# A recommendation kernel: every fourth early row gather waits for VectorE's count of products

## The chip, the cores and the metric

One core of one Trainium2 chip. The metric is the device time of one execution in microseconds (us). In the rows PE is TensorE, DVE VectorE, ACT ScalarE, POOL GpSimd, SP SyncE. The count of products is a semaphore, a counter that engines raise and wait for.

## What is computed

Rows of 32 embedding tables are gathered for 512 samples (32 fields of 16 numbers each), three layers of a compressed interaction network run on them, and a small tower of three matrix products follows. All is float32.

```python
e = jnp.stack([tbl_0[ids[:, 0]], ..., tbl_31[ids[:, 31]]], axis=1)      # 512 x 32 x 16
x0, xk, outs = e, e, []
for W in (W0, W1, W2):                                                  # 32 x 32 x 64, then 32 x 64 x 64
    xk = relu(einsum('bmd,bhd,mhk->bkd', x0, xk, W))
    outs.append(sum(xk, axis=2))
h = concatenate([concatenate(outs, axis=1), dense_ctx], axis=1)         # 512 x 208
h = maximum(h @ W_top1 + b_top1, 0)
h = maximum(h @ W_top2 + b_top2, 0)
y = h @ W_top3
```

## The kernel before

The batch is cut into eight pairs of 32-sample chunks; pair 0 is cut further, so that there are ten blocks (`BLOCKS`, line 32): blocks 0 and 1 have 256 columns (sample times dimension), block 2 has 512, blocks 3 to 9 have 1024. A step is (layer, block), and `BEGUN` (line 53) lists the 30 steps in the order in which they are begun. The program is written by hand for each engine, with semaphores between them.

GpSimd fetches the rows. One gather (`gather`, line 590) is one indirect DMA that brings 128 table rows of 16 numbers, one for each partition; 128 of them bring everything, 16 for each pair. Block 0 needs gathers 0 to 3, block 1 gathers 4 to 7, block 2 gathers 8 to 15, block 3 gathers 16 to 31, block 4 gathers 32 to 47, block 5 gathers 48 to 63, block 6 gathers 64 to 79. `gathered` has room for four pairs (`GRING`), so gather 64 waits for the last products of layer 0 on pair 0 (product 26, line 598). GpSimd issues 32 gathers at once (line 638) and then, by `GATHERS_IN` (line 70), 41 more ahead of its first multiplication, so gathers 0 to 72 stand one behind the other with no other wait than that of gather 64. Gathers 73 to 78 follow that first multiplication (`opposite_product` of block 4), and later ones are strewn between GpSimd's own products (line 631).

SyncE issues the plain DMAs in the order of `LOADS` (line 86). `scratch(b)` waits for the gathers of block b and copies their rows to DRAM (line 509); `field_tiles(b)` brings them back as eight tiles of four fields each, spread over partitions (line 557), which layers 1 and 2 multiply with. `layer0_operands(b)`, for blocks 4 to 9 only, brings the own and the rotated tiles for layer 0 (lines 522, 528, 535). `LOADS` has the copy and operands of block 5 ahead of the field tiles of block 4.

VectorE makes the products: one instruction multiplies one to three tiles by a factor (line 683; for layer 0 of blocks 0 to 3, called direct, lines 694 to 706) and writes them to `vz`, a ring of nine tiles. `VECTOR` lists all 139 products in order, and each raises `vz_ready` by one. "Product 4" is the one that raises it to 4. Products 1 to 4 are layer 0 of block 0, 5 to 8 layer 0 of block 1, 9 to 22 layer 1 of these two blocks, 23 to 26 layer 0 of block 2, 27 to 40 layer 2 of blocks 0 and 1, 41 to 47 layer 1 of block 2, 48 to 52 layer 0 of block 3, 53 to 59 layer 2 of block 2, 60 to 65 layer 1 of block 3, 66 and 67 layer 0 of block 4, which are the first on `rotated`. Product 73 is the first of layer 0 of block 5, product 75 the first that multiplies with the field tiles of block 4.

TensorE contracts the products with the weights (line 881) and raises `vz_used`, for which VectorE waits before it writes over a tile. For the first blocks TensorE also makes the factors. For the direct blocks it spreads the gathered rows over partitions in two waves (`spread_gathered`, line 848), between which it waits for a semaphore of its own, `wave_done`; it raises `factor_spread`, for which ScalarE (copy to `own`, line 754) and VectorE wait. For layers 1 and 2 it spreads the ReLU that ScalarE made of the accumulator (lines 826 and 779). There are three factor buffers.

Of the kernel before, what the change touches and what calls it, by code (L numbers as in the profile page):

```python
# [37 lines left out]
def stream(b):  # L38
    return BLOCKS[b][0] % STREAMS
# [7 lines left out]
def turn(b):  # L47
# [22 lines left out]
GATHERS_IN = {(0, 4): (41,), (2, 3): (6, 0), (0, 5): (5,), (1, 4): (0, 1, 3, 0, 0), (1, 5): (4, 0),  # L70
              (0, 6): (4,), (2, 4): (0, 1, 2, 1), (0, 7): (1,), (2, 5): (7, 0, 1, 0), (1, 6): (0, 0, 3),
              (1, 7): (1, 8), (2, 6): (4, 3, 0, 0, 0)}


SPLIT = {8: (3, 3, 2), 7: (3, 2, 2), 6: (3, 3), 5: (3, 2), 4: (2, 2), 3: (3,), 2: (2,)}
# [37 lines left out]
def pool_units(step):  # L113

    layer, b = step
    if layer == 0:
        return [(0, L0TILES)] if b not in DIRECT else []
    return [(1, t) for t in range(TILES - POOL_TILES[step], TILES)]
# [60 lines left out]
def vectors_to(step):  # L179

    return max(i for i, (of, _) in enumerate(VECTOR) if of == step) + 1
# [77 lines left out]
def pools_to(step):  # L259

    return max([i + 1 for i, (of, _) in enumerate(POOLS) if of == step], default=0)


def pools_used_to(step):
    return max([i + 1 for i, (of, _) in enumerate(POOLS_USED) if of == step], default=0)
# [81 lines left out]
def cin_dlrm(nc, table, ids, first_row, unit, turned, across, w0a, w0b, w0c, w1, w2, wt1, bt1, wt2,  # L347
             bt2, wt3, wt1_dense, dense, out):
    with ExitStack() as ctx:
# [6 lines left out]
        def sem(name):  # L356
            return ctx.enter_context(nc.semaphore(name))
# [60 lines left out]
        vz_ready, vz_used = sem("vz_ready"), sem("vz_used")  # L418
# [21 lines left out]
        def hidden_of(step, g):  # L440
            _, col, cols, _, _ = BLOCKS[step[1]]
            return hidden[stream(step[1])][:, g, col:col + cols]
# [9 lines left out]
        def quarter_rows(b):  # L452

            pair, _, _, first, rows = BLOCKS[b]
            return gathered[:, pair % GRING, first:first + rows, :].rearrange("p b d -> p (b d)")

        def operands_in(b):

            return 16 * sum(1 for a in range(b + 1) if a not in DIRECT and stream(a) == stream(b))

        def landed(b):

            return 16 * (turn(b) + 1)

        def relay_count(step):

            return 32 * sum(1 for of in BEGUN[:BEGUN.index(step) + 1] if of not in SPREAD and of[0]
                            and stream(of[1]) == stream(step[1]))
# [119 lines left out]
        @block.gpsimd  # L588
        def _(pool):
            def gather(i):  # L590
                pair, j = divmod(i, GATHERS)
                b = next(b for b, (of, _, _, first, rows) in enumerate(BLOCKS)
                         if of == pair and first <= j < first + rows)
                if j == 0 and pair >= GRING:
                    before = max(a for a in range(len(BLOCKS)) if BLOCKS[a][0] == pair - GRING)
                    for a in range(before):
                        if BLOCKS[a][0] == pair - GRING:
                            pool.wait_ge(vz_ready, vectors_to((0, a)))
                    pool.wait_ge(scratch_in[stream(before)][0], landed(before))
                    if before in DIRECT:  # L600
                        pool.wait_ge(vz_ready, vectors_to((0, before)))
                    else:
                        pool.wait_ge(scratch_in[stream(before)][1], operands_in(before))
                        pool.wait_ge(pz_ready, pools_to((0, before)))
                nc.gpsimd.indirect_dma_start(  # L605
                    gathered[:, pair % GRING, j, :], None, table,
                    bass.IndirectOffsetOnAxis(ap=index[:, i:i + 1], axis=0)).then_inc(rows_in[b], 16)

            def opposite_product(step):
                _, col, cols, _, _ = BLOCKS[step[1]]  # L610
                s, quarter = stream(step[1]), cols // QUART
                pool.wait_ge(opposite_in[s], operands_in(step[1]))
                if step[1] - 1 not in DIRECT:
                    pool.wait_ge(pz_used, pools_used_to((0, step[1] - 1)))
                nc.gpsimd.tensor_tensor(oz[:, 0:quarter], quarter_rows(step[1]), opposite[s][:, :],
                                        ALU.mult).then_inc(pz_ready, 1)

            def product(step, u):
                _, col, cols, _, _ = BLOCKS[step[1]]
                s = stream(step[1])  # L620
                g, t = pool_units(step)[u]
                if step[0] == 1:
                    pool.wait_ge(fields_in[s][t], landed(step[1]))
                if u == 0 and step in SPREAD:
                    pool.wait_ge(hidden_copied, COPIED.index(step) + 1)
                elif u == 0:
                    pool.wait_ge(relayed[s][g], relay_count(step))
                at = PLANE.index((step, u))
                if at >= PRING:
                    pool.wait_ge(pz_used, PRODUCT_USED[at - PRING])  # L630
                nc.gpsimd.tensor_tensor(pz[:, at % PRING, 0:cols], fields[s][:, t, col:col + cols],  # L631
                                        hidden_of(step, g), ALU.mult).then_inc(pz_ready, 1)

            pool.wait_ge(ids_in, 32)
            nc.gpsimd.tensor_tensor(index[:, :], ids_sb[:, :], first_sb[:, :].broadcast_to([P, PAIRS * GATHERS]),
                                    ALU.add).then_inc(index_ready, 1)
            pool.wait_ge(index_ready, 1)
            for i in range(FIRST_GATHERS):
                gather(i)
            sent = FIRST_GATHERS  # L640
            for step, u in POOLS:
                if step in GATHERS_IN:
                    for i in range(sent, sent + GATHERS_IN[step][u]):
                        gather(i)
                    sent += GATHERS_IN[step][u]
                if step[0] == 0:
                    opposite_product(step)
                else:
                    product(step, u)
            assert sent == PAIRS * GATHERS, sent  # L650
# [379 lines left out]
```

## Time and profile before

| | us |
|---|---|
| median of three runs | 450.08 (448.92 to 450.79) |
| the profiled execution | 448.99 |
| its span in the profile | 447.2 |
| TensorE busy with matmuls | 319.0 (71%), 1824 instructions |
| VectorE busy | 283.7 (63%), 174 instructions |
| GpSimd busy | 244.4 (55%), 189 instructions |
| ScalarE busy | 53.0 (12%), 71 instructions |

The span is what the profile's clock covers of the profiled execution; 1.8 us of the execution lie around it. No engine is busy all the time, so the share of busy time alone says little: one has to ask in which stretch an engine stands still, and for whom. In the profile a stretch on the chain that is called "issue" has no releaser that the records show, and "another core or an unknown queue" or "remote" stands where a semaphore moved late with no instruction beside it.

### The profile page before, as it was taken

What the parts mean: (1) busy time and instruction counts of PE and PEld (TensorE: products, weight loads), DVE (VectorE), ACT (ScalarE), POOL (GpSimd) and SP (SyncE); (2) the same over time, 40 slices, a digit from 0 to 9 for tenths busy, and PEclk for the clock granted to TensorE, in tenths of its full rate; (3) what the DMA queues carried; (4) which work ended last, traced back from release to release, by engine and by line L of the source; (5) the groups of instructions that cost most, each with busy time, mean ns of one, the idle gap of its engine ahead of it and who ended that gap; (6) DMA issues with size and microseconds to landing.
All of it is one profiled execution on the core that took longest, in us unless ns stands there. A gap on an engine that the chain in (4) does not pass through costs nothing.

```text
span 447.2 us, 4701 instructions
## 1 busy us (share of the span) xinstructions
PE 319.0 (71%) x1824; PEld 135.9 (30%) x1824; DVE 283.7 (63%) x174; ACT 53.0 (12%) x71; POOL 244.4 (55%) x189
## 2 busy tenths in 40 slices
PE   0300003039922999889899999899889996999997
PEld 0200002037611643423233333233223442333334
DVE  0000000006702767999999997999899976899911
ACT  1000000000000010101112212220112221122002
POOL 5777777300174000003887688997887928887300
PEclk9999999999985799999999999999999998999999
DMA  5434484000070004760387868979875899934000
GB/s 174 106 100 110 107 286 128 4 1 1 30 241 13 1 0 119 268 238 7 92 279 264 297 166 297 331 183 284 255 194 150 252 366 349 310 95 106 1 0 0
DMA packets 33104, 69.40 MB, mean 155 GB/s; under 512 B 5818, under 2 KB 14138, under 8 KB 33082
## 3 DMA queue, kind: packets, MB, share of 16 engines
q1 hardware_dynamic: 22074, 55.46, 37.6%
q10 hardware_dynamic: 6912, 12.59, 10.1%
q0 software_dynamic: 4096, 1.06, 2.6%
q8 instruction: 14, 0.23, 0.2%
q14 instruction: 8, 0.07, 0.0%
HBM read 54.40 MB, written 1.84 MB: 126 GB/s over the span
## 4 chain that ended last, share of the span: by engine, by line
PE 29%; issue 20%; DVE 17%; DMA 16%; another core or an unknown queue 10%; POOL 5%; SPq 1%; DVEq 1%; ACT 0%; ACTq 0%
PE acc L881 19%; DVE vz L683 16%; DMA fields_sb<-fields 10%; PE factor L848 4%; POOL gathered L605 3%; DMA fields<-gathered 2%; PE factor L826 2%; POOL pz L631 2%; DMA gathered<-in_table,index 2%; DMA rotated<-fields 1%; DVE feats L713 1%; PE factor L931 1%; SPq L557 1%; PE factor L913 1%
## 5 line engine op out<-in xcount | busy, mean ns | idle before, releaser
L881 PE MATMUL acc<-vz,w_sb 128*64 128x512 f32 (+2 forms) x1240 | 231.2, 512 | 34.0 <-DVE vz L683 18.7
L683 DVE TENSOR_TENSOR vz<-fields_sb,factor 128x3072 f32<-128x3072 f32 (+5 forms) x110 | 231.1, 2144 | 36.3 <-remote 18.8
L631 POOL TENSOR_TENSOR pz<-fields_sb,hidden 128x1024 f32<-128x1024 f32 x50 | 117.7, 2376 | 96.1 <-ACT hidden L762 67.8
L605 POOL DMA_INDIRECT gathered<-in_table,index x128 | 121.8, 952 | 73.4 <-DVE vz L683 37.3
L881 PEld LDWEIGHTS acc<-vz,w_sb 128*64 128x64 f32 x1240 | 87.6, 144 | 163.6 <-issue 118.4
L700 DVE TENSOR_TENSOR vz<-own,factor 128x256 f32<-128x256 f32 (+2 forms) x10 | 7.9, 794 | 75.5 <-issue 30.1
L848 PE MATMUL factor<-gathered,turned_sb 32*128 32x64 f32 (+2 forms) x128 | 15.7, 393 | 55.8 <-issue 51.7
L881 PE MATMUL acc<-pz,w_sb 128*64 128x512 f32 x200 | 50.2, 593 | 1.3 <-POOL pz L631 1.3
L748 ACT ACTIVATE factor<-hidden 128x1024 f32<-128x1024 f32 x24 | 24.6, 1027 | 89.4 <-DMA hidden<-relu_out 56.7
L779 ACT ACTIVATE relu_out<-acc 128x512 f32<-128x512 f32 (+2 forms) x30 | 15.3, 510 | 151.3 <-PE acc L881 110.1
L848 PE MATMUL factor<-gathered,unit_sb 32*128 32x64 f32 (+2 forms) x32 | 5.1, 407 | 33.6 <-remote 20.8
L848 PEld LDWEIGHTS factor<-gathered,turned_sb 32*128 32x128 f32 x128 | 10.8, 251 | 60.0 <-issue 53.2
L683 DVE TENSOR_TENSOR vz<-rotated,factor 128x2048 f32<-128x2048 f32 x12 | 26.9, 2280 | 2.3 <-issue 2.3
L881 PEld LDWEIGHTS acc<-pz,w_sb 128*64 128x64 f32 x200 | 15.1, 137 | 29.4 <-issue 25.0
L713 DVE TENSOR_REDUCE feats<-relu_out 128x32 f32<-128x512 f32 (+2 forms) x30 | 17.1, 571 | 5.0 <-ACT relu_out L779 5.0
L704 DVE TENSOR_TENSOR vz<-own,factor 128x512 f32<-128x512 f32 (+1 forms) x3 | 2.6, 863 | 22.7 <-remote 22.4
L754 ACT ACTIVATE own<-factor 128x256 f32<-128x256 f32 (+2 forms) x4 | 2.4, 598 | 108.0 <-PE factor L848 73.5
L848 PEld LDWEIGHTS factor<-gathered,unit_sb 32*128 32x128 f32 x32 | 3.2, 244 | 35.3 <-remote 21.0
L826 PE MATMUL factor<-relu_out,unit_sb 32*128 32x128 f32 (+2 forms) x64 | 11.6, 468 | 0.6 <-issue 0.6
L748 ACT ACTIVATE factor<-own 128x1024 f32<-128x1024 f32 x6 | 6.2, 1028 | 27.9 <-issue 20.3
L826 PEld LDWEIGHTS factor<-relu_out,unit_sb 32*128 32x128 f32 x64 | 5.3, 206 | 6.6 <-issue 6.3
L877 PE MATMUL acc<-oz,w0c_sb 128*64 128x256 f32 x48 | 6.3, 379 | 0.0
(34 smaller groups left out, 50.9 us busy)
## 6 DMA issues: line engine op xcount, KB each, us to landing
fields_sb<-fields SPq DMA_DIRECT2D x56, 512.0 KB
rotated<-fields SPq DMA_DIRECT2D x24, 512.0 KB
hidden<-relu_out ACTq DMA_DIRECT2D x48, 256.0 KB
own<-fields SPq DMA_DIRECT2D x6, 512.0 KB
gathered<-in_table,index POOLq DMA_INDIRECT x128
fields_sb<-fields SPq DMA_DIRECT2D x16, 128.0 KB
fields_sb<-fields SPq DMA_DIRECT2D x8, 256.0 KB
fields<-gathered SPq DMA_DIRECT2D x13, 128.0 KB
```

The lines of the kernel that those rows point to most:

```text
L557: sp.dma_start(fields[s][:, t, col:col + cols], each).then_inc(fields_in[s][t], 16)
L605: nc.gpsimd.indirect_dma_start(gathered[:, pair % GRING, j, :], None, table, bass.IndirectOffsetOnAxis(ap=index[:, i:i + 1], axis=0)).then ...
L631: nc.gpsimd.tensor_tensor(pz[:, at % PRING, 0:cols], fields[s][:, t, col:col + cols], hidden_of(step, g), ALU.mult).then_inc(pz_ready, 1)
L683: nc.vector.tensor_tensor(vz[:, at:at + nt, 0:cols].rearrange("p t (a n) -> p t a n", n=half), src[:, t:t + nt, col:col + cols].rearrange( ...
L700: nc.vector.tensor_tensor(vz[:, at, 0:cols].rearrange("p (a n) -> p a n", n=half), whole, slot_of(step, t), ALU.mult).then_inc(vz_ready, 1)
L713: nc.vector.tensor_reduce(feats[layer][:, pair, first:first + count], relu_of(step).rearrange("p (b d) -> p b d", d=DIM), op=ALU.add, axis ...
L748: nc.scalar.activation(factor_of(step, g), src.rearrange("p (a n) -> p a n", a=2), ACT.Copy).then_inc(factor_put, 1)
L779: nc.scalar.activation(relu_of(step), acc[:, n % 2, 0:half], ACT.Relu).then_inc(relu_done, 1)
L826: last = nc.tensor.matmul(factor_of(step, g)[:, ab, :], unit_sb[row:row + HROWS, :], relu_of(before)[row:row + HROWS, :], start=True, stop ...
L848: last = nc.tensor.matmul(slot_of(step, held)[:, ab, wave * quarter:(wave + 1) * quarter], by, rows[row, :], start=True, stop=True)
L877: last = nc.tensor.matmul(acc_of(step, q // 2)[:, part], w0c_sb[:, q, :], quarters, start=False, stop=q % 2 == 1)
L881: last = nc.tensor.matmul(acc_of(step, ab), w_sb[layer][:, kt, :], z[:, ab * half:(ab + 1) * half], start=start and j == 0, stop=stop and ...
```

## The change

A table `PACED` is added. In `gather`, ahead of the indirect DMA, GpSimd waits for VectorE's count of products where the gather's number is in the table: gather 12 for product 4, 16 for 7, 20 for 14, and so on to gather 68 for product 61. The order of all instructions stays.

```diff
+PACED = {12: 4, 16: 7, 20: 14, 24: 18, 28: 22, 32: 29, 36: 35, 40: 41, 44: 44, 48: 47, 52: 49, 56: 54, 60: 57, 64: 59,
+         68: 61}
 ...
                     else:
                         pool.wait_ge(scratch_in[stream(before)][1], operands_in(before))
                         pool.wait_ge(pz_ready, pools_to((0, before)))
+                if i in PACED:
+                    pool.wait_ge(vz_ready, PACED[i])
                 nc.gpsimd.indirect_dma_start(
                     gathered[:, pair % GRING, j, :], None, table,
                     bass.IndirectOffsetOnAxis(ap=index[:, i:i + 1], axis=0)).then_inc(rows_in[b], 16)
```

## Rows read from the trace of the kernel before

**Rows 1.** Page part 2: busy tenths in 40 slices of 11.2 us each.
```profile
PE   0300003039922999889899999899889996999997
...
DVE  0000000006702767999999997999899976899911
...
POOL 5777777300174000003887688997887928887300
```

**Rows 2.** Chain of work, in order of time: start us, us, what.
```profile
19.68 51.69 issue
...
75.21 20.79 another core or an unknown queue
...
122.89 11.83 another core or an unknown queue
134.78 8.46 another core or an unknown queue
```

**Rows 3.** Timeline of PE, ACT and DVE, 18 to 97 us: start, us, what, idle before.
```profile
18.56 1.12 PE L848 MATMUL factor<-gathered,turned_sb 32*128 32x64 f32 x12 [3.61 <-remote]
71.37 0.69 PE L848 MATMUL factor<-gathered,turned_sb 32*128 32x64 f32 x4 [51.69 <-issue]
...
96.04 0.48 PE L848 MATMUL factor<-gathered,unit_sb 32*128 32x64 f32 x2 [20.83 <-remote]
...
36.49 0.38 ACT L754 ACTIVATE own<-factor 128x256 f32<-128x256 f32 x1 [34.46 <-issue]
...
59.76 0.69 DVE L704 TENSOR_TENSOR vz<-own,factor 128x512 f32<-128x512 f32 x1 [22.35 <-remote]
```

**Rows 4.** Instructions of line 605, of 0 to 84, 121 to 141, 237 to 243 us.
```profile
L605 POOL DMA_INDIRECT gathered<-in_table,index x64: 940/945/1112, 4.1 to 83.0; - x64
...
L605 POOL DMA_INDIRECT gathered<-in_table,index x15: 943/947/985, 121.3 to 139.4; - x15
...
L605 POOL DMA_INDIRECT gathered<-in_table,index x4: 946/948/985, 237.8 to 241.6; - x4
```

**Rows 5.** Timeline of DVE: products 5 and 8, 30, 31, 59 to 61, 73 and 74.
```profile
97.69 0.42 DVE L700 TENSOR_TENSOR vz<-own,factor 128x256 f32<-128x256 f32 x1 [9.66 <-ACT own L754]
...
101.88 0.21 DVE L694 TENSOR_TENSOR vz<-gathered,factor 128x64 f32<-128x64 f32 x1
...
122.86 0.69 DVE L683 TENSOR_TENSOR vz<-fields_sb,factor 128x512 f32<-128x512 f32 x1 [0.57 <-PE acc L877]
134.74 0.95 DVE L683 TENSOR_TENSOR vz<-fields_sb,factor 128x768 f32<-128x768 f32 x1 [11.20 <-remote]
143.26 0.95 DVE L683 TENSOR_TENSOR vz<-fields_sb,factor 128x768 f32<-128x768 f32 x1 [7.56 <-remote]
...
182.65 7.74 DVE L683 TENSOR_TENSOR vz<-fields_sb,factor 128x1024 f32<-128x1024 f32 x3
...
223.54 4.47 DVE L683 TENSOR_TENSOR vz<-rotated,factor 128x2048 f32<-128x2048 f32 x2
```

**Rows 6.** Windows: length, PE, PEld, DVE, ACT, POOL busy, clock, DMA share, GB/s.
```profile
84.00:96.00 12.00, 0.00 (x0) 0.00 (x0) 0.55 (x2) 0.00 (x0) 0.00 (x0) 1.00 0.00 1
...
106.00:121.00 15.00, 14.28 (x192) 10.72 (x188) 11.20 (x18) 1.17 (x4) 0.00 (x0) 1.00 0.01 3
...
143.30:151.00 7.70, 6.73 (x56) 5.60 (x56) 5.39 (x9) 0.28 (x1) 0.00 (x0) 0.53 0.01 2
151.00:190.50 39.50, 35.70 (x262) 16.94 (x262) 32.86 (x28) 3.59 (x6) 0.00 (x0) 1.00 0.34 112
```

**Rows 7.** Timeline of DVE beside short rows of gathers: products 77 to 80, 104.
```profile
235.65 12.07 DVE L683 TENSOR_TENSOR vz<-fields_sb,factor 128x2048 f32<-128x2048 f32 x4
...
316.24 3.35 DVE L683 TENSOR_TENSOR vz<-fields_sb,factor 128x3072 f32<-128x3072 f32 x1 [1.35 <-DMA fields_sb<-fields]
```

**Rows 8.** Timeline of SP's queue: rotated tiles of block 5, field tiles of block 4.
```profile
173.91 6.07 SPq L535 DMA_DIRECT2D rotated<-fields  x4
...
183.94 11.05 SPq L557 DMA_DIRECT2D fields_sb<-fields  x8
```

## The prediction

> **What bounds the kernel now.** I read the page's 40 slices first [rows 1]. The reader is to see that TensorE and VectorE are nearly empty in the first nine slices (0 to 100 us), thin again in the slices around 130 us, and full from about 150 us to the end, while GpSimd is busy in just the empty places. The second view is the chain of work [rows 2]: it names four stretches in which nothing on the chain works: 51.69, 20.79, 11.83 and 8.46 us, together 92.8 us of the 447.2 us span. The third is the timeline of those stretches [rows 3]. Block 0 has its rows early, and TensorE finishes the 12 spreading matmuls for products 2 and 3 at 19.68 us. But ScalarE's copy, which waits for the spread done before those, starts at 36.49 us, VectorE's product 2 at 59.76 us, and TensorE itself goes on at 71.37 and 96.04 us. All these wait for a count that TensorE raised long before: 40 us before, for product 2.
>
> What runs meanwhile is the row of gathers. 64 are issued back to back from 4.1 to 83.0 us, one each 1.25 us (79 us over 63 steps), and 15 more from 121.3 to 139.4 us [rows 4]. The second row of gathers brings the second standstill: product 30 starts at 122.86, product 31 at 134.74, product 32 at 143.26 us [rows 5]. TensorE's signals come through only some time after the gathers end: 96.04 minus 83.9 is 12.1 us after 80 us of gathers, 143.26 minus 140.4 is 2.9 us after 19 us of them, in both cases 15%. In the first of these tails, 84 to 96 us, neither DMA nor any engine is busy [rows 6], so it isn't the loads. And in 151 to 190.5 us, where there are loads (112 GB/s) but no gather, TensorE is busy 35.7 of 39.5 us [rows 6]. So I read: a long unbroken row of gathers holds back what TensorE signals to the other engines and to itself. From 151 us on the kernel is bound by VectorE and TensorE together, and whatever the first 61 products gain should move to the end.
>
> **The change part by part.** It adds 15 waits on GpSimd, ahead of gathers 12, 16, ... 68, and removes nothing. Behind each wait on GpSimd's queue stand all later gathers and, behind gather 72, the first opposite product. The long row of 64 becomes a row of 12, then 15 groups: 14 of four and a last of eleven (68 to 78). Each group starts when VectorE has finished product 4, 7, 14, ... 61. The wait as an instruction I price at nothing: GpSimd has idle time after every group.
>
> I add up when product 61 ends; before, that is 182.65 + 7.74 = 190.4 us [rows 5].
> - Until product 4: gather 11 ends at 4.1 + 11 x 1.25 + 0.95 = 18.8 us; a tail of 15% of 15 us gives 21.0. Then ScalarE's copy and products 1 to 4, whose spreads are half made. The same four products of block 1 take from 97.69 to 102.09, 4.4 us with the spreads between [rows 5]; I take 3.5. Product 4 ends at 24.5 us.
> - Products 5 to 61 without gathers: 96.04 [rows 3] to the stall at 122.9 is 26.5 us, 143.26 to 190.4 is 47.1 us, and products 30 and 31 between need some 3.5 us (two of 0.7 and 0.95 us and the ReLU between): 77 us.
> - The groups. One has four issues, 5.0 us, with its tail 5.75 us. The upper bound is 5.75: every signal held from the first gather to the tail's end and nothing running beside it. For the lower bound I look at short rows of gathers later on: the four at 237.8 to 241.6 us [rows 4] fall into a run of four products without a gap [rows 7], so their price is nothing, and eight from 310 us cost 1.35 us before product 104 [rows 7]. Those products last 3.3 us and the ring of nine tiles holds three of them; the early ones last 0.7 to 1.2 us, so VectorE has only some 2 to 3 us of work in stock. A group should cost between 5.75 - 2.45 = 3.3 us where products are short, and 2.2 us from the blocks of 512 columns on, if the signals are held throughout; I take these. Two groups (products 4 and 7), where everything hangs on TensorE's spreads, get 3.5 each. 7 + 5 x 3.3 + 7 x 2.2 = 39 us for the 14 groups of four, and 5 us for the last group of eleven, near the eight at 310 us but with more gathers. The ends for the 14 are 14 x 0 and 14 x 5.75 = 80 us. I am nearer to the middle than to the late rows, because in the second standstill VectorE stood still from 123.55 us, 2.3 us after its first gather [rows 4, 5].
> - TensorE's clock. After the second standstill the granted clock is low: 0.53 over 143.3 to 151.0 us, that is mostly the lower level of 1.2 GHz [rows 6]. With a pause per group, more of the early stretch may run there. TensorE is busy 14.3 of 15 us in 106 to 121 and 35.7 of 39.5 us later [rows 6]; if all that were at 1.2 GHz, it would cost up to 50 us; if VectorE stays the slower one, nothing. I take 12, since the pauses are short and, where TensorE is slow, its stock of tiles lasts through a group.
>
> Sum: 24.5 + 77 + 39 + 12 + 5 = 157.5 us against 190.4: 33 us less. Profiled execution before: 448.99 us; 448.99 - 33 = 416. It stood 1.1 us below the median of three (450.08), so I say 417.
>
> Where the gain goes later: it stays if loads keep up. Gathers 60 to 63 now wait for product 57, about the time of product 59. On SyncE's queue the copies of their rows, the own and rotated loads of block 5 (6.07 us of issues and some landing, about 10) and the eight field tiles of block 4 (11.05 us) stand one behind the other [rows 8]. So the rotated tiles are there about 20 us and the fields about 31 us after product 59 began. Before, the first product on the rotated tiles starts at 223.54 us, 41 us after product 59, and the fields are wanted at 228.0, 45 us after [rows 5]. 14 us are left, so this costs nothing. Block 2 needs gathers 8 to 15, which come after product 4 and are wanted at product 23; block 3 needs 16 to 31, which are out after product 22 and wanted at 48.
>
> A rule that speaks against the change: the Trainium skill, "SBUF — State Buffer", section "Who interferes with whom", says that only VectorE and GpSimd share ports and that TensorE and ScalarE never wait on anyone. By it the gathers would not be the cause, and the pacing would bring nothing. The trace shows ScalarE and TensorE standing still beside the gathers; it is about signals, not ports, and so the rule may hold and still not decide this. It is rival four.
>
> **Rivals.**
> 1. Short groups are free, as in the late rows. The 14 cost 1 us each, 14 us, the clock 4, the last group 3: 24.5 + 77 + 14 + 4 + 3 = 122.5, which gives 450 - 68 = 382 us at best. With 2 us each, clock 8: 140.5, 400 us. For it: four gathers at 237.8 us cost nothing. Against: early products are short and signals many.
> 2. Slower: each group holds back everything for its 5.75 us. 24.5 + 77 + 14 x 5.75 + the last group 11 x 1.25 x 1.15 = 16 + clock 12 = 210 us, 20 us later than before: 470 us. It decides from a price of (190.4 - 24.5 - 77 - 12 - 5) / 14 = 5.1 us a group. For it: in the rows of 64 and 15 almost nothing ran beside the gathers. Against: late short rows, and that VectorE has tiles in stock.
> 3. The early gain comes, but is partly eaten behind product 61: by the clock (30 us in place of 12), or by SyncE's queue if the 14 us of slack are used up. 432 to 446 us.
> 4. The stalls have another cause than the row of gathers (a slow start of the program, the loads on SyncE's queue). The early stalls stay and the waits fall where GpSimd had slack (it has nothing to do from about 145 to 200 us [rows 1]): 450 us. Against: two stalls of different length, both ending 15% after their gathers.
>
> **How the numbers follow.** Forecast, 404 to 431 us: 0.50. Rival 1, 382 to 404: 0.22. Rival 3: 0.12. Rival 2: 0.10. Rival 4: 0.06. The likeliest gives 417 us. The range leaves out the best part of rival 1 and rival 2: 394 to 446 us. A measurement of this kernel can tell some 0.5% from no change; faster by more than that: 0.84, within: 0.05, slower: 0.11.
>
> **What would show it.** In the changed kernel ScalarE's first copy should start near 21 us, product 4 end near 25, product 61 near 150; the four dead stretches of the chain should be gone and gaps of 2 to 4 us stand beside each group of four. The span from product 61 to the end should be as before (256.8 us) within some us. It is wrong if product 2 still waits until gather 11 is long over, if gaps per group are above 5 us, or if the granted clock stays at half up to product 59.

## The result, and the profile after

| | before | after |
|---|---|---|
| median, us | 449.5 (447.9 to 450.8, four runs) | 400.0 (399.0 to 402.0, four runs) |
| profiled execution, us | 448.99 | 402.0 |
| its span, us | 447.2 | 400.2 |

The ratio is 0.891, with a 95% interval of 0.886 to 0.895: 49.5 us, or 11%, faster. Here and below a time is the median of all executions; in some of them a kernel runs slower at a lower granted clock, and a ratio leaves these out.

From the page of the kernel after, part 2: busy tenths in 40 slices, here of 10.0 us each.

```profile
PE   0358839796399299989999989997899999799997
...
DVE  0013523468149399999999899979999986989810
...
POOL 5633342337335556798849888978996396797000
PEclk9999965869599779999999999999999999899999
```

Where TensorE and VectorE had nine nearly empty slices [rows 1], they now work in every slice from the third on, with holes at slices 6, 11 and 14 (50 to 60, 100 to 110 and 130 to 140 us), and GpSimd's work is spread thin up to 150 us. The granted clock is low in part of slices 6 to 15; over 52 to 73 us it is 0.52, that is mostly the lower level of 1.2 GHz (window, its length, then busy time of PE, PEld, DVE, ACT, POOL, clock, DMA share, GB/s):

```profile
52.00:73.00 21.00, 15.20 (x100) 10.26 (x102) 7.38 (x11) 0.87 (x2) 6.45 (x8) 0.52 0.18 53
```

The chain of work of the kernel after, all stretches of over 1.5 us, from the start of the spreads to product 61, in which nothing on it works (start us, us, what):

```profile
15.07 2.33 another core or an unknown queue
18.56 2.75 another core or an unknown queue
26.50 3.09 another core or an unknown queue
32.12 8.49 another core or an unknown queue
50.09 6.20 another core or an unknown queue
76.69 1.68 another core or an unknown queue
97.38 2.73 another core or an unknown queue
101.25 6.00 another core or an unknown queue
...
131.89 7.39 issue
```

These answer to [rows 2]: 40.7 us in nine pieces where there were 92.8 us in four (and 3.56 us more at 14.95 us, which [rows 2] leaves out). The seven pieces behind product 4 are 35.6 us. On the chain "dead" doesn't mean that no engine works: in the last piece VectorE makes product 60 for 3.35 us, and without it the seven are 32.2 us.

The timeline of VectorE in the kernel after: products 1, 4, 5, 6; then 13, 20 to 22, 48, 60 and 61, 62 to 65.

```profile
21.48 0.42 DVE L706 TENSOR_TENSOR vz<-own,factor 128x256 f32<-128x256 f32 x1 [14.00 <-ACT own L760]
...
23.04 0.21 DVE L700 TENSOR_TENSOR vz<-gathered,factor 128x64 f32<-128x64 f32 x1
26.91 0.42 DVE L706 TENSOR_TENSOR vz<-own,factor 128x256 f32<-128x256 f32 x1 [3.66 <-PE factor L854]
30.79 0.69 DVE L710 TENSOR_TENSOR vz<-own,factor 128x512 f32<-128x512 f32 x1 [3.46 <-PE factor L854]
...
40.73 0.95 DVE L689 TENSOR_TENSOR vz<-fields_sb,factor 128x768 f32<-128x768 f32 x1 [2.44 <-remote]
...
56.31 2.42 DVE L689 TENSOR_TENSOR vz<-fields_sb,factor 128x768 f32<-128x768 f32 x3 [6.22 <-remote]
...
108.62 1.22 DVE L706 TENSOR_TENSOR vz<-own,factor 128x1024 f32<-128x1024 f32 x1 [8.70 <-PE factor L854]
...
135.79 3.35 DVE L689 TENSOR_TENSOR vz<-fields_sb,factor 128x3072 f32<-128x3072 f32 x1 [5.76 <-remote]
140.08 3.35 DVE L689 TENSOR_TENSOR vz<-fields_sb,factor 128x3072 f32<-128x3072 f32 x1 [0.94 <-remote]
...
143.69 11.01 DVE L689 TENSOR_TENSOR vz<-fields_sb,factor 128x2048 f32<-128x2048 f32 x4
```

Product 4 ends at 23.25 us and product 61 at 143.4 us, against 190.4 us [rows 5]: 47.0 us earlier, which is the whole difference of the two profiled executions (448.99 - 402.0). From product 61 to the end of the span it is 256.8 us in both.

The gathers, by the instructions of their line in four stretches of the kernel after (name, count, duration in ns, first and last start in us):

```profile
L611 POOL DMA_INDIRECT gathered<-in_table,index x8: 943/946/947, 44.9 to 53.7; - x8
...
L611 POOL DMA_INDIRECT gathered<-in_table,index x12: 943/947/948, 90.2 to 104.0; - x12
...
L611 POOL DMA_INDIRECT gathered<-in_table,index x12: 942/945/948, 123.0 to 136.7; - x12
...
L611 POOL DMA_INDIRECT gathered<-in_table,index x11: 943/947/986, 143.7 to 156.9; - x11
```

The groups did not stay groups of four: gathers 12 to 67 went out as nine rows and not fourteen. Where the products outran the gathers, the next count was already there when GpSimd came to it: gathers 20 to 27 are one row of eight, 40 to 51 and 56 to 67 rows of twelve. VectorE's three largest gaps (6.22, 8.70 and 5.76 us) lie beside just these three. Beside the last row, of eleven, VectorE makes four large products without a gap. Beside a row of four it can be as if no gather ran. These are products 50 and 51 and product 53 of the kernel after, beside gathers 52 to 55 (115.0 to 119.7 us), and the same three of the kernel before, where no gather runs; the idle time before them is the same:

```profile
115.87 2.35 DVE L706 TENSOR_TENSOR vz<-own,factor 128x1024 f32<-128x1024 f32 x2 [1.19 <-PE factor L854]
...
120.03 1.22 DVE L689 TENSOR_TENSOR vz<-fields_sb,factor 128x1024 f32<-128x1024 f32 x1 [1.23 <-PE factor L832]
...
169.71 2.35 DVE L700 TENSOR_TENSOR vz<-own,factor 128x1024 f32<-128x1024 f32 x2 [1.19 <-PE factor L848]
...
173.87 1.22 DVE L683 TENSOR_TENSOR vz<-fields_sb,factor 128x1024 f32<-128x1024 f32 x1 [1.23 <-PE factor L826]
```

### The profile page after: what moved, and what is told of

Read it like the earlier page. It is cut to its first block, busy times and chain, and to the rows that moved or that the text cites. A ratio compares the mean times of both kernels' runs of the same rounds, so it can differ in the third digit from the quotient of the medians.

```text
span 400.2 us, 4701 instructions
## 1 busy us (share of the span) xinstructions
PE 332.2 (83%) x1824; PEld 143.6 (36%) x1824; DVE 284.2 (71%) x174; ACT 53.2 (13%) x71; POOL 244.5 (61%) x189
## 4 chain that ended last, share of the span: by engine, by line
PE 38%; POOL 17%; DMA 16%; issue 10%; another core or an unknown queue 8%; DVE 8%; SPq 1%; ACTq 1%; ACT 0%; DVEq 0%; POOLq 0%
PE acc L887 26%; POOL gathered L611 9%; DMA fields_sb<-fields 9%; POOL pz L637 8%; DVE vz L689 7%; PE factor L854 5%; PE factor L832 2%; DMA fields<-gathered 2%; DMA gathered<-in_table,index 2%; DMA rotated<-fields 1%; DMA hidden<-relu_out 1%; PE factor L937 1%; PE factor L919 1%; ACTq L796 1%
## 5 line engine op out<-in xcount | busy, mean ns | idle before, releaser
L887 PE MATMUL acc<-vz,w_sb 128*64 128x512 f32 (+2 forms) x1240 | 240.1, 529 | 32.2 <-DVE vz L689 19.4
L887 PEld LDWEIGHTS acc<-vz,w_sb 128*64 128x64 f32 x1240 | 91.8, 150 | 165.8 <-issue 123.3
L854 PE MATMUL factor<-gathered,turned_sb 32*128 32x64 f32 (+2 forms) x128 | 18.4, 447 | 15.0 <-remote 14.3
L689 DVE TENSOR_TENSOR vz<-rotated,factor 128x2048 f32<-128x2048 f32 x12 | 26.9, 2282 | 1.3 <-ACT factor L754 1.3
L854 PEld LDWEIGHTS factor<-gathered,turned_sb 32*128 32x128 f32 x128 | 12.5, 288 | 19.9 <-remote 15.6
L832 PE MATMUL factor<-relu_out,unit_sb 32*128 32x128 f32 (+2 forms) x64 | 12.9, 525 | 2.1 <-ACT relu_out L785 2.1
```

What stands on the lines that cost most here:

```text
L689: nc.vector.tensor_tensor(vz[:, at:at + nt, 0:cols].rearrange("p t (a n) -> p t a n", n=half), src[:, t:t + nt, col:col + cols].rearrange( ...
L832: last = nc.tensor.matmul(factor_of(step, g)[:, ab, :], unit_sb[row:row + HROWS, :], relu_of(before)[row:row + HROWS, :], start=True, stop ...
L854: last = nc.tensor.matmul(slot_of(step, held)[:, ab, wave * quarter:(wave + 1) * quarter], by, rows[row, :], start=True, stop=True)
L887: last = nc.tensor.matmul(acc_of(step, ab), w_sb[layer][:, kt, :], z[:, ab * half:(ab + 1) * half], start=start and j == 0, stop=stop and ...
```

## The experiments

Each set of runs had the kernel before beside it on its own chip. On four chips that took 448.8, 451.0, 450.3 and 451.1 us; on a fifth, where e1 to e4 ran, it took 353.5 us. So each result is given with the time of before that belongs to it. I call a chip one "with the standstill" where before takes about 450 us.

### One wait alone (e1, e7)

```diff
-PACED = {12: 4, 16: 7, 20: 14, ..., 68: 61}
+PACED = {12: 4}
```

> Of the fifteen waits only the first is kept: gather 12 waits for product 4, and gathers 12 to 63 follow in one row. My theory (the stall grows with the length of the unbroken row of gathers): products 1 to 4 are done at 23 us as in the changed kernel, then 52 gathers of 1.25 us run to 88 us and their tail of 15% to 98 us, so product 61 ends near 192 us and the time is 448 to 455 us, no gain at all. Rival (the early stall is one of the program's start, and it is enough that the first products get through): near the changed kernel, 400 to 415 us.

Measured: 352.3 us against 353.5, ratio 0.999 (0.991 to 1.007). Both theories had counted on a kernel before of 450 us. From the windows of e1 (length, then busy time of PE, PEld, DVE, ACT, POOL, clock, DMA share, GB/s) and its row of gathers:

```profile
15.00:93.00 78.00, 73.39 (x690) 45.96 (x686) 57.73 (x70) 6.51 (x15) 58.88 (x63) 1.00 0.57 169
...
L610 POOL DMA_INDIRECT gathered<-in_table,index x73: 941/947/1114, 4.1 to 94.3; - x73
```

73 gathers stand in one row at 1.25 us each, as in [rows 4], and TensorE is busy 73.4 of 78 us beside them. Product 61 ends at 93.2 us. On this chip the row of gathers holds back nothing.

The same kernel was then run on a chip that has the standstill.

> The kernel of e1 again, for a chip where the kernel before takes about 450 us: only gather 12 waits (for product 4), the 52 gathers behind it follow in one row. Theory R (a row at 1.25 us a gather outruns a drain of 1.44 us, and only gaps in the row clear it): products 1 to 4 done at 23 us, the next standstill until about 98 us, 445 to 455 us, no gain. Rival (it is enough that the program's start gets through before the long row): 400 to 415 us. Where before takes 353 us: 352 us as in e1.

Measured: 443.6 us against 451.0, ratio 0.988 (0.983 to 0.993): a gain of some 5 us, and a time 1.4 us below my range, but nowhere near the rival's 400 to 415 us. VectorE's timeline in e7: products 4, 6, 7, 9 to 13, and the row of gathers.

```profile
23.45 0.21 DVE L699 TENSOR_TENSOR vz<-gathered,factor 128x64 f32<-128x64 f32 x1
...
34.84 0.69 DVE L709 TENSOR_TENSOR vz<-own,factor 128x512 f32<-128x512 f32 x1 [6.96 <-remote]
90.59 0.42 DVE L705 TENSOR_TENSOR vz<-own,factor 128x256 f32<-128x256 f32 x1 [55.06 <-remote]
...
97.67 3.34 DVE L688 TENSOR_TENSOR vz<-fields_sb,factor 128x512 f32<-128x512 f32 x5 [6.53 <-remote]
...
L610 POOL DMA_INDIRECT gathered<-in_table,index x52: 940/944/947, 23.9 to 87.6; - x52
```

Product 4 is done at 23.7 us, as in the kernel after, and then the long row brings the standstill back: VectorE starts product 6 at 34.8 and product 7 at 90.6 us. It clears at 97.67 us, 9.1 us after the last gather's end (88.55), 14% of the row's 64.7 us. A start that gets through is not enough; the row has to be broken up all along.

### Rows of eight and of two (e2, e3, e8)

```diff
-PACED = {12: 4, 16: 7, 20: 14, 24: 18, 28: 22, ...}
+PACED = {12: 4, 20: 14, 28: 22, 36: 35, 44: 44, 52: 49, 60: 57, 68: 61}            # e2
+PACED = {12: 4, 14: 5, 16: 7, 18: 10, 20: 14, 22: 16, 24: 18, ..., 68: 61, 70: 62}   # e3, e8
```

> Every second wait is kept: rows of 12, seven of 8 and a last of 11 gathers. My theory: a group of eight lasts 10 us and 1.5 us of tail, VectorE has 2 to 3 us of work in stock, so it costs 8 to 9 us, seven of them 60 us, where the fourteen groups of four and the clock together cost 43 us in the changed kernel. Product 61 ends 10 to 20 us later than there: 410 to 420 us. Rival (each gather costs the same wherever it stands): as the changed kernel, 400 us within 4.

> A wait at every second gather from 12 to 70, the counts between those of the change put halfway. My theory: the signals are held only from some 2.3 us after the first gather of a row on, and a pair lasts 2.5 us, so a pair costs under 1 us; 28 pairs cost 20 us or less where the changed kernel lost 43 us: 375 to 388 us. Rival (each gather costs the same wherever it stands): 400 us within 4. Rival that a group costs a fixed price by its start and tail: slower than the changed kernel, 410 us or more.

Measured, on the chip without the standstill: e2 353.4 us, ratio 1.003 (0.995 to 1.011); e3 353.3 us, ratio 1.003 (0.995 to 1.011). There these waits cost and bring nothing that can be told from no change. They tell nothing of the theory, which is about the other chips. On one of those:

> The kernel of e3 again: a wait at every second gather. Where before takes about 450 us, theory R: pairs leave a shorter queue than groups of four, so each signal waits less; 375 to 390 us. Rival (the drain's 1.44 us a gather is what counts, however the gathers are grouped): 396 to 404 us, as the changed kernel. Where before takes 353 us: 353 us as in e3.

Measured: 395.8 us against 451.0, ratio 0.880 (0.866 to 0.894). My 375 to 390 us was wrong, and what I called the rival (396 to 404) was nearer: the time lies just below it. That is hardly better than the changed kernel. But the pairs did not stay pairs either: gathers 12 to 67 went out as sixteen rows, among them one of eight (gathers 40 to 47) and one of ten (56 to 65), and VectorE's two largest gaps lie beside these two. The gathers of both rows, and products 46, 60 and 61:

```profile
L610 POOL DMA_INDIRECT gathered<-in_table,index x8: 941/947/947, 85.5 to 94.3; - x8
...
L610 POOL DMA_INDIRECT gathered<-in_table,index x10: 943/946/947, 115.9 to 127.1; - x10
...
97.11 1.75 DVE L688 TENSOR_TENSOR vz<-fields_sb,factor 128x1536 f32<-128x1536 f32 x1 [6.60 <-remote]
...
130.13 6.62 DVE L688 TENSOR_TENSOR vz<-fields_sb,factor 128x3072 f32<-128x3072 f32 x2 [7.20 <-remote]
```

So e8 is not a test of pairs, and it doesn't show whether the price goes by the gather or by the length of a row.

### The changed kernel again (e5, e11)

> The changed kernel itself, beside the kernel before. In the runs of e1 to e4 the kernel before took 353 us on its chip and not 450, and its first products ran beside the unbroken row of gathers. Theory S (the standstill beside a long row of gathers comes and goes with the chip or its state; the change helps only where it is): where the kernel before takes about 353 us, the changed one takes 350 to 358 us; where before takes about 450, this takes about 400. Rival (the change costs something where there is no standstill, since gathers come later and SyncE's loads behind them): 360 us or more where before takes 353.

> The changed kernel once more, on whatever chip this is. Where before takes 353 us: 351 to 356 us, no change, as the waits of e2 and e3, which lie on both sides of it, changed nothing there. Where before takes 450 us: 396 to 404 us.

Measured: 401.1 us against 448.8, ratio 0.890 (0.882 to 0.897), and 400.2 us against 450.3, ratio 0.888 (0.882 to 0.894). Both fell on chips with the standstill. On the chip without it the changed kernel was not run; e2 and e3, with half and with twice as many waits, changed nothing there.

### No wait for VectorE, but slower gathers (e4, e6, e12, e9)

These are the kernel before, with a small fill behind each of the first 73 gathers. The loads, the order and the number of gathers are those of before, and the row is unbroken.

```diff
+                if 0 < i <= 73:
+                    pool.wait_ge(filled, i)
                 nc.gpsimd.indirect_dma_start(
 ...
+                if i < 73:
+                    nc.gpsimd.memset(pz[:, 3, 0:256], 0.0).then_inc(filled, 1)     # 256 in e4, e6; 384 in e12; 512 in e9
```

> The kernel before, without waits for VectorE, but each of the first 73 gathers is followed by a small fill of 256 columns on GpSimd (0.3 to 0.5 us with its wait), so that gathers come each 1.6 to 1.75 us in place of 1.25 us, in one unbroken row. Theory R (rate): the tail of 15% says that something behind the gather drains them at 1.44 us each; gathers slower than that leave no backlog, TensorE's signals come through from the start, product 61 ends at 110 to 140 us and the time is 370 to 400 us. Theory L (length: as long as gathers follow each other the signals are held, at whatever rate): the row lasts until 110 us, product 61 ends near 210 us, 465 to 475 us.

Measured: 361.9 us against 353.5, ratio 1.023 (1.013 to 1.033), on the chip without the standstill. Product 61 ends there at 94.9 us, against 93.2 to 94.4 us in e1 to e3; most of what is lost comes later, as the next paragraphs show for e9.

> The kernel of e4 again: the first 73 gathers in one row, a fill of 256 columns behind each. Where the kernel before takes 353 us: 362 us as in e4, nothing new. Where it takes about 450: theory R (a drain that takes 1.44 us a gather, so slower gathers leave no backlog) 365 to 400 us; theory L (an unbroken row holds the signals at whatever rate) 460 us or more.

> As e6 with a fill of 512 columns: the fill of 256 took 0.33 us and gave a gather each 1.55 us; this should give one each 1.75 us. Theory R with queueing (at 1.55 us the drain of 1.44 us is 93% busy and signals still waited 1 to 4 us; at 1.75 us it is 82% busy): where before takes 450 us, product 61 ends at 115 to 128 us in place of 141, and the time is 376 to 390 us, if the later gathers (63 at 115 us) do not hold the loads. Rival (the signals wait for each gather by itself, not for a queue): 396 us or more. Where before takes 353 us: 365 to 375 us, since only the lateness of the gathers is left.

> As e6 and e9 with a fill of 384 columns behind each of the first 73 gathers: one each 1.65 us, between 1.55 (398 us, product 61 at 141 us) and 1.76 (378 us, product 61 at 96 us). Theory R, with a drain of 1.44 us a gather by the tails of 15%: most of the queueing is gone, product 61 ends at 98 to 110 us and gather 63 comes 7 us earlier than in e9: where before takes 450 us, 370 to 376 us. If the drain is really slower, between 1.55 and 1.75 us a gather, part of the standstill stays: 380 to 395 us. Where before takes 353 us: 362 to 368 us.

Measured, all on chips with the standstill; the gap from one gather to the next is (last start - first start) / (count - 1) of the rows below:

| | us from gather to gather | product 61 ends, us | time, us | before, us | ratio (95%) |
|---|---|---|---|---|---|
| before | 1.25 | 190.4 | 449.5 | | |
| e6 | 1.56 | 141.0 | 398.4 | 448.8 | 0.884 (0.877 to 0.891) |
| e12 | 1.67 | 97.7 | 370.4 | 451.1 | 0.823 (0.816 to 0.830) |
| e9 | 1.76 | 95.9 | 378.1 | 451.0 | 0.845 (0.836 to 0.854) |

```profile
L608 POOL DMA_INDIRECT gathered<-in_table,index x73: 949/952/1113, 4.1 to 116.3; - x73
...
L608 POOL DMA_INDIRECT gathered<-in_table,index x69: 952/952/1152, 4.1 to 117.7; - x69
...
L608 POOL DMA_INDIRECT gathered<-in_table,index x64: 949/949/1116, 4.1 to 115.2; - x64
```

These are e6, e12 and e9. The three differ in the length of the fill alone. The early standstill is gone at 1.67 us: product 61 ends within 5 us of e1's. At 1.56 us a part is left. So the pace of the gathers decides and not the loads, and the limit lies between 1.56 and 1.67 us. The plain picture behind my expectation, a drain of 1.44 us a gather, was too fast: at 1.56 us nothing should have been left of it. For e9 it had the time right by luck: product 61 ended 19 us before the earliest that I had named (115 us), and about as much was lost behind it.

The windows of the stretch from product 4 to 61, of the kernel after, of e6 and of e9 (columns as above):

```profile
23.10:143.20 120.10, 86.62 (x670) 53.92 (x669) 57.07 (x68) 6.33 (x14) 52.95 (x56) 0.81 0.35 104
...
19.00:140.90 121.90, 89.55 (x674) 57.38 (x670) 58.03 (x69) 6.35 (x14) 87.32 (x135) 0.80 0.44 136
...
18.00:96.00 78.00, 72.20 (x676) 44.95 (x674) 56.80 (x69) 5.41 (x13) 65.76 (x90) 1.00 0.40 121
```

The same products take 120 us in the kernel after and 78 us in e9. For the same matmuls TensorE is busy 86.6 us at a mean granted clock of 0.81 in the one, and 72.2 us at the full clock in the other: so at most 14.4 us of the difference is the clock, and the rest is waiting.

What limits e9 then is seen in its timeline (VectorE's sum behind product 69, ScalarE's ReLU that this sum waits for, GpSimd's gather 72 and its first product):

```profile
136.46 0.69 DVE L718 TENSOR_REDUCE feats<-relu_out 128x32 f32<-128x512 f32 x1 [16.67 <-issue]
...
135.83 0.60 ACT L784 ACTIVATE relu_out<-acc 128x512 f32<-128x512 f32 x1 [22.24 <-PE acc L882]
...
131.53 0.95 POOL L608 DMA_INDIRECT gathered<-in_table,index  x1 [0.27 <-POOL pz L612]
...
132.98 0.73 POOL L620 TENSOR_TENSOR oz<-gathered,opposite 128x256 f32<-128x256 f32 x1
```

VectorE stands still for 16.67 us, because the opposite product of block 4 is queued behind gather 72, which the fills have delayed to 131.5 us. In e12 this gap is 7.5 us. That is what a slower pace costs, and why e12 at 1.67 us beats e9 at 1.76 us, and why e4 is slower than before where there is no standstill to remove.

### Slow gathers first, fast ones later (e10)

As e9, with the fill behind the first 48 gathers only.

> As e9, but only the first 48 gathers have the fill of 512 columns behind them; the others come each 1.25 us. In e9 product 61 ended at 95.7 us, free of stalls, and then VectorE waited for the late gathers (63 at 115 us; product 73 ended at 155 us, against 128 us on the chip of e1). Here gather 63 comes at about 108 us and meets products of 2 to 3 us. Theory R: where before takes 450 us, 368 to 374 us. Rival (a row of 16 and more at 1.25 us brings the standstill back even there): 380 us or more. Where before takes 353 us: 358 to 366 us.

Measured: 387.2 us against 450.3, ratio 0.854 (0.847 to 0.861). My 368 to 374 us was wrong. VectorE's timeline in e10, products 62 and 63 to 65, and the gathers from 48 on.

```profile
105.99 2.28 DVE L688 TENSOR_TENSOR vz<-fields_sb,factor 128x2048 f32<-128x2048 f32 x1
133.56 8.82 DVE L688 TENSOR_TENSOR vz<-fields_sb,factor 128x3072 f32<-128x3072 f32 x3 [25.30 <-remote]
...
L608 POOL DMA_INDIRECT gathered<-in_table,index x31: 941/945/985, 88.8 to 127.0; - x31
```

The long row at 1.25 us (25 gathers, and six more 0.6 us later) brings a gap of 25.3 us among products of up to 3.35 us. Large products do ride over short rows, as in [rows 7] and beside the row of eleven in the kernel after, but not over this one of 31.

## Why the prediction was right, and where it was not

- What bounds the early stretch (TensorE's signals are held beside the gathers) was right: e7 brings the standstill back with the row, and e12 and e9 take it away by slower gathers (e6 in part). Rival 4, another cause, falls with these: e7's start got through and the standstill came back, and the loads on SyncE's queue were the same. That queue was slow in the kernel before (the eight field tiles of block 2 took 15.40 us of it from 40.10 us on, and 6.40 us in e1), but in e7 the same eight took 7.48 us from 32.47 us on, while TensorE's signals were held. What I couldn't see from one trace is that four of the five chips have it and one has not. The rule of the Trainium skill, "SBUF — State Buffer", section "Who interferes with whom", that TensorE and ScalarE never wait on anyone, fits the chip of e1: TensorE is busy 73.4 of 78 us beside the gathers there. On the other four TensorE's signals came late, and no run shows whether a port of the SBUF has a part in it.
- That it is TensorE's signals and not all of them can be read from the kernel before. Beside its first row ScalarE's copy ends at 36.87 us, and VectorE's product 1, which waits for it, starts at 36.98 us. Beside its second row product 31 ends at 135.69 us [rows 5], and TensorE's matmuls on it start at 135.75 us. So ScalarE's and VectorE's signals came within 0.11 us in these two places, where TensorE's for product 2 took 40 us.

```profile
36.98 0.42 DVE L700 TENSOR_TENSOR vz<-own,factor 128x256 f32<-128x256 f32 x1 [29.08 <-issue]
...
135.75 1.55 PE L881 MATMUL acc<-vz,w_sb 128*64 128x128 f32 x12 [9.34 <-issue]
```

- Until product 4: 24.5 us forecast, 23.25 us measured.
- Products 5 to 61 without gathers: 77 us forecast (96.04 to 122.9 is 26.9 us and not 26.5, so its terms add up to 77.5); e9, where nothing was held, has 77.6 us (18.25 to 95.9).
- The 14 groups, 39 us, and the clock, 12 us: together 51 us forecast. The kernel after needs 120.2 us for these products, so 42.6 us are left for both. By the chain 32.2 to 35.6 us of them are dead stretches, without or with product 60, and 7.0 to 10.4 us are left for the clock; the busy times allow it 14.4 us at most. So the groups took 32 to 36 us where I had 39, or 2.3 to 2.5 us for each of the 14 in place of 2.8, and the clock 7 to 10 us where I had 12. Both were priced somewhat too high. The step that failed is "if the signals are held throughout": beside gathers 52 to 55 VectorE waited no longer than without gathers. One more thing was wrong and partly evened that out: the groups did not stay groups of four, which I never asked of the counts, and the rows of eight and twelve carry the large gaps. Whether a group, a gather or a row's length has the price, no run separates.
- The last group: 5 us forecast, nothing measured. The sum has it at the wrong place too: this group waits for product 61, so it could not have delayed it. Four products run beside it in 11.0 us without a gap.
- What follows product 61: no loss forecast, none measured (256.8 us in both). The queue of SyncE had its slack.
- The sum: 33 us forecast for the profiled execution, 47.0 us measured; product 4 gives 1.3 us of the difference, the groups and the clock 8.4 less the 0.6 us that the products took more, the last group 5, and the rest is rounding. The time, 400.0 us, is in the range. It lies below the forecast's own 404 to 431 us and in rival 1's 382 to 404 us, to which I had given 0.22. Rival 1's picture, short groups free as in the late rows, did not come about: at 2.3 to 2.5 us the groups are nearer to the forecast's 2.8 than to free. That the time meets its dearer sum (2 us a group, 8 us of clock: 400 us) is in part luck, since product 4 came earlier and the last group was free.
- Rival 2 (slower, from 5.1 us a group on) is far off, at 2.3 to 2.5 us. Rival 3 didn't come about: nothing was eaten behind product 61.
- The signs that I had named: ScalarE's first copy near 21 us came at 20.99 us, and product 61 near 150 us at 143.4 us. The gaps of 2 to 4 us beside each group did not come so: three are above 5 us, each beside two or three groups that had run together, while beside gathers 52 to 55 there is none.

## What to carry to other kernels

If an engine's record shows no work and its consumers start long after its last instruction, look at what GpSimd issues meanwhile: unbroken indirect gathers can hold back TensorE's semaphore signals, and spacing them evenly (here one each 1.67 us in place of 1.25) was worth more than pausing between bursts (370 us against 400). It has its price where there is no standstill: with one each 1.56 us e4 took 2.3% longer. Before tuning around a stall of this kind, measure on several chips, because the same kernel took 353 us on one chip and 450 us on four. A wait that paces by another engine's count paces only as long as that engine is the slower one; check in the trace that groups stay groups.

## What the runs showed of the hardware that I had not expected

- One and the same kernel took 448.8 to 451.1 us on four chips and 353.5 us on a fifth. Each chip was measured at one time only, so whether the standstill belongs to the chip or to the state that it was in is not shown, nor what differs.
- On the four, the pace decides within a narrow band: with a gather each 1.56 us product 61 ended at 141.0 us, with one each 1.67 us at 97.7 us. Whether the number of descriptors, the DMA's own signals or something else in a gather is what takes the time wasn't tried. Nor was it separated whether the fill and its wait do anything but take time.
- After a row the signals stay held for a time that grows with the row, some 15% of it: 12.1 us after 80 us, 9.1 us after 65 us (e7), 5.7 us after 39 us (e10, 127.9 to 133.56 us), 2.9 us after 19 us.
- Beside the two rows of the kernel before, where TensorE's signals were late, one of ScalarE's and one of VectorE's came within 0.11 us.
